# Moving the fp16 high-half copy of an attention kernel's value tiles from VectorE to ScalarE

## What is computed

```python
q = lat @ Wq                                   # 4 batches x 1024 queries, 16 heads of 64
kv = concatenate([ctx, lat], axis=1) @ Wkv     # 1024 + 154 = 1178 keys
k, v = split(kv, 2, axis=-1)
attn = softmax(einsum('bhid,bhjd->bhij', q, k) * scale)
out = einsum('bhij,bhjd->bhid', attn, v)       # then @ Wout, + x, layernorm, gate, experts
```

## Time and profile before

| | |
|---|---|
| time, median of 3 runs | 2211.45 us (2210.63 to 2211.83) |
| the profiled execution | 2209.7 us, span on the core 2208.0 us |
| TensorE busy | 2021.2 us, 92% of the span |
| VectorE busy | 1632.3 us, 74% |
| ScalarE busy | 1472.4 us, 67% |
| GpSimd busy | 1421.1 us, 64% |
| TensorE's granted clock, mean | 0.974 |

### The profile page before, as it was taken

The page is one execution under the profiler, slowest core; times in us unless marked ns, Lnnn a source line. Parts: engine busy times, 40 slices in busy tenths (PEclk is TensorE's granted clock), DMA queues, the critical chain, the costliest instruction groups (busy, mean ns, idle before and its releaser), DMA issues. The chain is left out here.

```text
span 2208.0 us, 63023 instructions
## 1 busy us (share of the span) xinstructions
PE 2021.2 (92%) x25468; PEld 1367.9 (62%) x25468; DVE 1632.3 (74%) x3111; ACT 1472.4 (67%) x1831; POOL 1421.1 (64%) x803
## 2 busy tenths in 40 slices
PE   2799999999999999999999999999999997679997
PEld 2266666667666666667666665676666655556675
DVE  7677777776778888867788888767888883645554
ACT  4277777775777777666777776657777767245664
POOL 3088887783787887755777787738878777022332
PEclk9699999999999999999999999999999998889999
DMA  4122222222222222222222222222222221271110
GB/s 164 37 52 53 63 53 60 60 52 53 64 52 57 58 52 52 53 51 66 60 60 53 53 52 53 47 70 52 63 53 53 60 48 33 92 295 39 43 43 26
DMA packets 127504, 137.92 MB, mean 62 GB/s; under 512 B 45537, under 2 KB 92309, under 8 KB 126069
## 3 DMA queue, kind: packets, MB, share of 16 engines
q1 hardware_dynamic: 123477, 124.49, 21.9%
q0 software_dynamic: 3744, 9.39, 1.4%
HBM read 53.06 MB, written 26.15 MB: 36 GB/s over the span
## 5 line engine op out<-in xcount | busy, mean ns | idle before, releaser
L693 POOL TENSOR_TENSOR probs_split<-probs,probs_split 128x1024 f16<-128x1024 f32 x576 | 1222.6, 2134 | 380.5 <-ACT probs_split L778 379.5
L771 ACT ACTIVATE probs<-score 128x1024 f32<-128x1024 f32 (+1 forms) x640 | 655.5, 1024 | 414.4 <-PE score L1060 403.3
L915 DVE TENSOR_REDUCE max_parts<-aux 128x1 f32<-128x512 f32 x1024 | 682.7, 688 | 97.4 <-PE aux L1060 89.0
L778 ACT ACTIVATE probs_split<-score 128x1024 f16<-128x1024 f32 (+1 forms) x640 | 652.6, 1020 | 0.0
L1154 PE MATMUL acc<-values,probs_split 128*128 128x65 f16 x5120 | 555.5, 193 | 7.6 <-POOL probs_split L693 7.4
L1158 PE MATMUL acc<-values,probs_split 128*128 128x64 f16 x4608 | 520.4, 194 | 0.0
L1159 PE MATMUL acc<-values,probs_split 128*128 128x65 f16 x4608 | 518.3, 192 | 0.0
L1154 PEld LDWEIGHTS acc<-values,probs_split 128*128 128x128 f16 x5120 | 464.5, 97 | 65.5 <-POOL probs_split L693 11.1
L1060 PE MATMUL aux<-k_high,q_both 128*128 128x512 f16 (+1 forms) x1536 | 462.6, 335 | 44.6 <-DVE values L911 20.5
L1060 PE MATMUL score<-q_both,k_high 128*128 128x512 f16 (+1 forms) x1280 | 486.7, 380 | 9.5 <-DMA q_max<-max_row 7.2
L1060 PE MATMUL score<-q_max,k_low 65*128 65x512 f16 (+1 forms) x1280 | 489.4, 382 | 0.0
(11 more groups left out here) (166 smaller groups left out, 2267.3 us busy)
## 6 DMA issues: line engine op xcount, KB each, us to landing
k_high<-raw SPq DMA_DIRECT2D x128, 147.2 KB, 2.5
q_both<-raw SPq DMA_DIRECT2D x128, 128.0 KB, 2.5
piece_in<-in_L_ffn_W SPq DMA_DIRECT2D x64, 256.0 KB, 3.2
halves<-piece_out SPq DMA_DIRECT2D x128, 128.0 KB, 2.4
k_low<-raw SPq DMA_DIRECT2D x64, 147.2 KB, 2.4
q_max<-raw SPq DMA_DIRECT2D x64, 128.0 KB, 2.5
w<-halves SPq DMA_DIRECT2D x16, 512.0 KB
w<-halves SPq DMA_DIRECT2D x8, 1024.0 KB
```

What stands on the lines that cost most here:

```text
L693: nc.gpsimd.tensor_tensor(out=low[0:r, :], in0=prob(h, j)[0:r, :], in1=high[0:r, :], op=ALU.subtract)\
L771: nc.scalar.activation(prob(h, j)[0:r, :], score[j % 2][0:r, :], ACT.Exp, scale=SCALE)\
L778: nc.scalar.activation(halves(h, j)[0][0:r, :], score[j % 2][0:r, :], ACT.Exp, scale=SCALE)\
L915: nc.vector.tensor_reduce(max_parts[g % 2][:, t, c:c + 1], bank[:, :], AX.X, ALU.max)\
```

## The change

In the steps that have a "v" chunk, ScalarE copies the bank to the high half between the two exponentials of its score tile; VectorE waits for that copy and only subtracts. The wait for `av_done`, which protects the older values in the same buffer, moves along with the copy. The four chunks ahead of the loop go to ScalarE too, ahead of its first exponentials.

```diff
+            def value_high(chunk):
+                _, pair, g = chunk
+                act.wait_ge(aux_full, NUMBER[chunk] + 1)
+                if g == 0:
+                    at_least(act, av_done, 2 * JT * 2 * (pair - 1))
+                nc.scalar.activation(value_half(pair, g, 0), value_bank(bank_of(chunk), g), ACT.Copy).then_inc(values_high, 1)
+
             def head(h):
                 for j in range(JT):
                     of, jj = tile_ahead(h, j)
                     if of < HEADS:
                         exponent(of, jj)
+                    for chunk in BESIDE[h][j]:
+                        if chunk and chunk[0] == "v":
+                            value_high(chunk)
+                    if of < HEADS:
                         high_half(of, jj)
...
+            for chunk in BEFORE:
+                if chunk[0] == "v":
+                    value_high(chunk)
             for j in range(AHEAD):
                 exponent(0, j)
                 high_half(0, j)
...
                 elif kind == "v":
                     dve.wait_ge(aux_full, number + 1)
-                    if chunk[2] == 0:
-                        at_least(dve, av_done, 2 * JT * 2 * (g - 1))
-                    nc.vector.tensor_copy(value_half(g, chunk[2], 0), value_bank(bank, chunk[2])).then_inc(values_high, 1)
                     dve.wait_ge(values_high, len(VALUE_TILES) * g + chunk[2] + 1)
```

## The result

The changed kernel takes 2200.51 us, the median of 5 runs (2196.57 to 2202.65), against 2211.45 (2209.53 to 2212.85) of the kernel before on the same chip: ratio 0.9944, 95% interval 0.9934 to 0.9955, 10.9 us less. The forecast was 2200.5. The profiled execution took 2202.65 us, its span on the core is 2200.9.

The account below looks back on a forecast made before the run. TensorE was taken as the bound, so only its waits count. Profiled 2209.7 us - 16.2 + 6.1 = 2199.6, or 2201.35 against the median 2211.45; forecast 2200.5 with the three heads' extra, range 2192 to 2209.

Parts of the forecast that it names:

- Step 7, the gain of 16.2 us: In each head's seventh step, ScalarE's copy hides while VectorE is busy; the subtraction starts earlier, ending TensorE's next-step waits: 16.2 us gained.
- step 8: The place where TensorE's maximum matmul waits for the previous step's subtraction: 0.22 to 0.39 us per head, forecast to vanish.
- Step 5, the loss of 6.1 us: In each head's fifth step VectorE waits for the chunk, so the copy is exposed: 0.34 us lost per odd plain head.
- The copy at 0.37 and 0.48 us: ScalarE's time per copy of a "v" chunk: 0.37 us for two tiles, 0.48 for three, from L1394 and L802.
- Queued behind the copy, at no cost: On ScalarE the second exponential starts 0.4 to 0.5 us later, delaying GpSimd; costed at nothing, 50 us if cover were gone.
- The three heads that choose experts … gain a little more: In three heads where VectorE is behind, a little extra gain; used to say 2200.5 instead of 2201.35 us.
- The nine heads with a late DMA, 2.8 us: Nine heads whose scores wait for the maxima's DMA were assumed to have no wait to remove: 2.8 us less gain.
- A dearer copy: Rival: ScalarE's copy is dearer or later where exposed, 6.2 us per 0.1 us, up to 2211.7 us; chance 0.13.
- The gain swallowed at step 8: Rival: TensorE, arriving earlier, waits for VectorE's maximum instead, leaving only the loss: 2217.5 us; chance 0.06.
- Table loads: Rival: the copy needs another function table than the exponential, two 1.283 us loads per chunk: 2280 us or more; chance 0.02.
- No loss at step 5: Rival: ScalarE's copy begins before its exponential drains, or the nine DMA waits fall otherwise: 2190 to 2195 us; chance 0.09.

## Why the prediction was right

*Step 7, the gain of 16.2 us.* Right. The copy takes the second exponential's place and lies in VectorE's shadow, the subtraction comes earlier, and TensorE's waits at step 8, 16.9 us by their sum over the trace, are gone in all classes of heads. With the chunks of step 7 alone the kernel is 19.8 us faster, the three heads' 7.7 (-8.8 and +1.1 behind them) included; the 12.1 left for the other heads are less than the 15.0 that the term gives them (16.2 less three times 0.39), and head 0, of which more below, is 1.8 of what is missing.

*Step 5, the loss of 6.1 us.* Right in its place and mechanism, short in size: 9.4 us, of which 8.0 by the medians of the classes. The odd plain heads lose 0.375 us instead of 0.34. ScalarE began the copy 0.92 us behind the exponential's start, as forecast from the earlier trace rows; the copy took 0.38 and not 0.37 us; and from its end to the subtraction's start it was 0.11 us (595.99 to 596.10), above the upper end of the 0.04 to 0.10 of the prediction, which had them from VectorE waiting for itself and TensorE waiting for VectorE. The odd gated heads, forecast at nothing, lose 0.04, and the even plain ones lose 0.02 where 0.02 were to be gained: the same 0.04. The other 1.4 us are the five heads in which ScalarE or the hand-over came late; where VectorE copies for itself, their waits at step 5 are like the others'.

*The copy at 0.37 and 0.48 us.* Right, 0.38 and 0.48 to 0.49. Of the two figures that were weighed, L1394's held. The estimate of 0.51 and 0.62 us by the Trainium skill (ScalarE: Activation LUTs, Rules for kernel authors) came from a figure that is stated for an ACTIVATE with a bias pointer; these copies have none, so it was not the figure for them, and their times do not contradict the page.

*Queued behind the copy, at no cost.* Right: GpSimd's waits for the second exponential fell, and TensorE waited for GpSimd's halves 9 times in both kernels, for 7.4 us before and 6.9 after.

*"The three heads that choose experts … gain a little more".* This term was mis-sized: 0.85 us in the sum, -8.1 us in these heads and +2.4 behind them in the trace, 4 to 5 by the runs without them. What failed is the idea that VectorE gains there what it gains elsewhere; it also moved out of GpSimd's way, and 3.2 us of the 8.1 are the clock of two heads. The row with 1.44 us for 32 columns stands in the trace of the kernel before, and no term of the prediction came from it.

*The nine heads with a late DMA, 2.8 us.* About right. In the profiled execution before they are 3, 5, 6, 9, 12, 26, 29, 40 and 54; in eight of them there was no wait at step 8 to be removed, in head 29 one of 0.17 us, as the prediction assumed. Seven of them wait in every profiled execution of this study (all but 5 and 29), and these gained 2.7 us less than their classes' medians.

*Partly luck.* The forecast, with its 2.8 us for the DMA, gives the ordinary heads -9.2 us; they made -5.6. Of the 3.6 missing, head 0 has 1.8 (it is 1.1 and 1.2 us longer also in the two kernels that leave its chunks as they were, so most of this lies with the one execution before), four heads at step 5 have 1.2, and 0.6 are the heads 11 and 33, unexplained. The three heads and those behind them, for which the forecast comes to -1.9, made -5.7. These two misses cancel almost to the digit: 2200.51 against 2200.5 is closer than the terms were.

*The rivals.* A dearer copy: no, though the price of 6 us per 0.1 us was right. The gain swallowed at step 8: no wait for a maximum came in its place; TensorE's waits for maxima fell from 15.3 to 11.1 us over the whole span. Table loads: none added. No loss at step 5: refuted by the kernel with step 5 alone.

## What to carry to other kernels

A copy handed to another engine is judged place by place: where its old engine was late, the move gains, where that engine stood waiting for the input, the move loses the new engine's queue and the hand-over; keep both halves apart and take the better one. An engine's instruction whose duration in the trace is many times that of its like is worth a look at what another engine ran in that moment: a changed order on one engine gave 4 to 5 us here, where the gain and the loss of the work moved came to 5 to 7. When a forecast and a result agree, compare the terms too.

## What was not expected of the hardware

VectorE's small instructions between SBUF tiles took eight to nine times their usual time beside GpSimd's subtractions: 0.17 to 1.44 us for 128x32, 0.22 to 2.08 for 128x64. It is shown for the copy that the order on VectorE alone switches this on and off; that it is the shared pair of ports rests on the page of the Trainium skill named above and on the slow copy's end at GpSimd's own end.

Behind a stretch of 1.6 us in which TensorE stood still, its granted clock was at 1.2 GHz for most of the next 3.8 us in heads 28 and 44, and at 2.4 GHz all through in head 60 behind a stretch of the same length. With step 5 alone on ScalarE the same wait brought the clock down in head 60 and not in the other two; with the copy behind the second exponential a wait of 1.5 us did so in none. What makes the difference was not found.
